# Local attention: transposes ahead of the scores and the projection ahead of the values on the tensor engine

## The reference, cut to what matters

```
q = rmsnorm((x @ wq.T).reshape(B, T, 16, 64), q_norm_w)
k = rmsnorm((x @ wk.T).reshape(B, T, 4, 64), k_norm_w)
v = (x @ wv.T).reshape(B, T, 4, 64)
scores = q . k / sqrt(64), -inf where not (i >= j and i - j < 64)
y = softmax(scores) . v
x = x + y.reshape(B, T, 1024) @ wo.T      # the x on the right of @ above is layernorm(x)
```

## Time and profile before

| what | us |
|---|---|
| median of 3 runs | 2483.01 (2477.14 to 2483.77) |
| the profiled execution, its own time | 2484.49 |
| its span, first to last instruction | 2482.6 |
| PE busy | 2057.6 (83%) |
| DVE busy | 1849.0 (74%) |
| POOL busy | 1429.4 (58%) |
| ACT busy | 1399.7 (56%) |
| local attention, first projection to last addition to x | 1523.9 to 2058.0 |

### The profile page before, as it was taken

How to read it: one execution, slowest core, us unless ns; L and a number is a source line. 1 busy time by engine, 2 the same in 40 slices (tenths; PEclk the granted TensorE clock), 3 DMA queues, 4 the chain that set the end, 5 groups by cost and what they waited for, 6 DMA issues and landing times. The chain is left out here.

```text
span 2482.6 us, 44194 instructions
## 1 busy us (share of the span) xinstructions
PE 2057.6 (83%) x13760; PEld 1290.2 (52%) x13760; DVE 1849.0 (74%) x2871; ACT 1399.7 (56%) x2582; POOL 1429.4 (58%) x1094
## 2 busy tenths in 40 slices
PE   3888888888888886999865894888888888999486
PEld 1334443334333333677643783555555556777476
DVE  5999999999999997577644343777887775776545
ACT  4657676666666662466543452555555564665254
POOL 4788888777888886233244464455555543332646
PEclk7999999999999999799987897999999998999588
DMA  4222222222222221200111220000000001000342
GB/s 121 74 76 72 75 77 73 71 73 70 73 72 75 76 74 43 73 11 11 31 39 50 82 82 27 10 9 8 8 8 8 5 1 56 11 11 7 133 155 73
DMA packets 104423, 130.71 MB, mean 53 GB/s; under 512 B 33668, under 2 KB 65718, under 8 KB 103632
## 3 DMA queue, kind: packets, MB, share of 16 engines
q1 hardware_dynamic: 95600, 111.19, 15.4%
q0 software_dynamic: 8192, 17.59, 2.0%
q10 hardware_dynamic: 512, 0.53, 0.1%
HBM read 111.16 MB, written 25.20 MB: 55 GB/s over the span
## 5 line engine op out<-in xcount | busy, mean ns | idle before, releaser
L829 POOL TENSOR_TENSOR m_hc<-m_h,m_cs 128x1024 f32<-128x1024 f32 x256 | 602.6, 2358 | 183.1 <-DVE m_h L739 167.8
L739 DVE TENSOR_TENSOR_SCAN m_h<-m_da,m_pdb 128x1024 f32<-128x1024 f32 x256 | 585.2, 2286 | 27.5 <-DVE m_pdb L711 3.9
L432 PE MATMUL m_py<-m_hc,ident 128*128 128x512 f32 x1024 | 506.2, 618 | 1.9 <-POOL m_hc L829 1.9
L614 ACT ACTIVATE m_da<-m_dt,m_aneg 128x508 f32<-128x508 f32 x512 | 331.7, 709 | 118.1 <-DVE m_h L739 102.6
L711 DVE TENSOR_TENSOR m_pdb<-m_du,m_pdb 128x1024 f32<-128x1024 f32 x256 | 309.1, 1207 | 26.6 <-PE m_pdb L419 17.5
L432 PEld LDWEIGHTS m_py<-m_hc,ident 128*128 128x128 f32 x1024 | 200.2, 198 | 222.8 <-issue 214.3
L1082 ACT ACTIVATE x_prT<-x_pt 77x512 f32<-77x512 f32 x256 | 138.0, 586 | 139.3 <-PE x_pt L984 138.6
L2077 POOL TENSOR_TENSOR d_r<-d_mean_sq,minus_half 128x20 f32<-128x20 f32 x32 | 113.6, 3549 | 171.7 <-DVE d_mean_sq L2048 171.7
L1198 POOL TENSOR_TENSOR x_kd<-x_kT,x_hm 128x308 f32<-128x308 f32 x64 | 45.0, 703 | 278.5 <-ACT x_v_raw L1094 278.5
L419 PE MATMUL m_pdb<-m_bcrow,m_sel 96*128 96x512 bf16 x256 | 101.2, 396 | 112.6 <-DVE m_h L739 112.6
L2069 POOL TENSOR_TENSOR d_pr<-d_pr,d_rden 128x512 f32<-128x512 f32 x128 | 130.4, 1039 | 49.9 <-DVE d_rden L1991 49.9
(11 more groups left out here) (308 smaller groups left out, 4541.0 us busy)
## 6 DMA issues: line engine op xcount, KB each, us to landing
m_cs<-crow SPq DMA_DIRECT2D x256, 256.0 KB, 3.1
f_row<-f_sorted SPq DMA_DIRECT2D x24, 400.0 KB, 3.3
c_row<-c_sorted SPq DMA_DIRECT2D x40, 144.0 KB
d_back<-c_routed SPq DMA_DIRECT2D x32, 128.0 KB
f_sorted<-in_F_blank SPq DMA_DIRECT2D x9, 400.0 KB
cw_gud<-in_C_gud SPq DMA_DIRECT2D x1, 3456.0 KB
x<-in_x SPq DMA_DIRECT2D x8, 256.0 KB, 4.8
fw_w<-in_F_w SPq DMA_DIRECT2D x1, 2048.0 KB, 8.5
```

The source lines that it names most:

```text
L432: ins = mm(py[:, c, :], S.ident[:, :], hc[n % BUF][:, c, :], start=False, stop=n == NS - 1)
L614: A_(dst, src, ACT.Exp, scale=aneg[:, d, c, n:n + 1]).then_inc(s["da_ready"], 1)
L739: V.tensor_tensor_scan(h[n % BUF][:, way], da[n % BUF][:, d:d + CH * GT][:, way], pdb[:, b:b + 2, :].rearrange("p c t -> p (c t)")[:, way] ...
L829: P.tensor_tensor(hc[n % BUF][:, :, :], h[n % BUF][:, :].rearrange("p (c t) -> p c t", c=CH), bc(cs[n % BUF][:, :], 1, CH), ALU.mult).then ...
```

## The change

On PE, in every slot, the code of slot 2 (transposes of queries and keys) and of slot 3 (projection) moves up to stand right behind the turn. In slot 2 the order is now turn, transposes, scores, values; it was turn, scores, values, transposes. In slot 3 it is now turn, projection, values; it was turn, values, projection. Slots 0 and 1 keep their order. Waits move with the blocks to which they belong. No instruction is added or removed, and the other engines' code is untouched.

```diff
                     nxt, m, n, o = (b.plus(k) for k in (1, 2, 3, -1))
-                    if nxt.real() and q % 2 == 0:
-                        scores(nxt, q // 2)
-                    if q == 1 and n.real():
...
-                    last = b if q else o
-                    if last.real():
-                        values(last, (q - 1) % NQ)
-                    if q == 1 and o.real():
...
                     if q == 2 and m.real():
                         pe.wait_ge(s["qn_ready"], 2 * (m.n + 1))
...
                         mm(pkv[:, :], xT[:, :], W.wkv[:, :], start=True, stop=True).then_inc(s["qkv_mm"], 1)
+                    if nxt.real() and q % 2 == 0:
+                        scores(nxt, q // 2)
+                    if q == 1 and n.real():
...
+                    last = b if q else o
+                    if last.real():
+                        values(last, (q - 1) % NQ)
+                    if q == 1 and o.real():
...
```

More of the change, by code:

```diff
@@ L1903, in slot @@
                         mm(pkv[:, :], xT[:, :], W.wkv[:, :], start=True, stop=True).then_inc(s["qkv_mm"], 1)
+                    if nxt.real() and q % 2 == 0:
+                        scores(nxt, q // 2)
+                    if q == 1 and n.real():
+                        pe.wait_ge(s["xh_ready"], n.n + 1)
+                        if due(n.n - 4):
+                            pe.wait_ge(s["x_ready"], n.n - 4)
+                        tr(px[:, 0:T], xh[:, 0, :], S.ident[:, :]).then_inc(s["t_mm"], 1)
+                    last = b if q else o
+                    if last.real():
+                        values(last, (q - 1) % NQ)
+                    if q == 1 and o.real():
+                        pe.wait_ge(s["cT_ready"], NQ * (o.n + 1))
+                        if due(o.n):
+                            pe.wait_ge(s["x_ready"], o.n)
+                        if n.real():
+                            pe.wait_ge(s["xT_ready"], n.n + 1)
+                        for i in range(NP):
+                            ins = mm(px[:, T:2 * T], cT[o.p][:, i, :], W.wo[:, i, :], start=i == 0, stop=i == NP - 1)
+                        ins.then_inc(s["o_mm"], 1)
                 walk_sequences(pe, slot, 5)
```

## The result

The changed kernel takes 2447.59 us in the median of 4 runs (2442.64 to 2449.27), the kernel before 2480.60 us beside it: a ratio of 0.9864, 95% interval 0.9842 to 0.9886, so 33 us less, with about 5 us to either side. The direction and the mechanism were as forecast; the size was not: 2459 was named, with a range of 2451 to 2469. The profiled execution went from 2484.49 to 2447.85 us, its span from 2482.6 to 2446.0. Where the 36.6 us are, by the two traces: 33.0 in the 28 periods, 2.2 in the start of the layer, 0.5 at its end, and the remaining 1 us outside it.

A forecast was written before the change was run, and what follows sets the result against it. A loop through several engines, none full, was taken as the bound: 15.89 us per period, to become 14.98. Saved 25.5, less 1.1 at the start, plus 0.4 at the end: 24.8 us, so 2458.2, named 2459; range 2451 to 2469.

The forecast's parts named there:

- the 28 periods: One layer's PE order, repeating once per sequence, from the mark behind projection 3 to that behind 31; 15.89 us each before.
- The loop of 7.15 + 8.72: Old period: 7.15 us from mark to slot 2's turn, released by POOL, then 8.72 of PE to the next mark.
- "DVE finishes it at 1793.01, +8.19": DVE finishes `qn` 8.19 us after the mark, so PE's transposes start at +8.29 after a new 0.65 us wait.
- PE's marks: Mark E: on PE, the start of the turn that follows a projection; the periods are counted between these.
- the forecast of 14.98: New period in us: 8.29 + 1.37 + 1.62 + 0.58 + 0.44 + 2.68, which is 0.91 less than 15.89.
- the 25.5 predicted: Saving in us over the periods between marks 3 and 31: 28 x 0.91.
- Hand-over of 0.10 and blocks of 6.69: DVE's `qn` to PE's transposes takes 0.10 us; PE's blocks from the transposes' start to the next mark take 6.69.
- Cover of the copies, of the exponential and of `top`: `qT`/`kT` copies out at +10.52, before the projection at +12.30; exponential 0.55 us in hand; `top`'s delay absorbed by DVE idle time.
- Start +1.1: Layer's start costs 1.1 us: first projection about 2.0 late (bounds +1.3 to +3.9), about 0.9 given back before mark 3.
- End: One more wait for `cT` goes outside the 28 periods: -0.4 us, bounds 0 and -0.9.
- The clock: Rival: new waits lower PE's clock in the loop; 3 periods cost 20 us, all 28 cost 162 more; chance 0.02.
- 2458.2: Forecast median in us: 2459.7 for the profiled execution, less 1.5 because the runs' median is that much below it.

The follow-up runs named there:

- The two halves done alone: Kernel before with only slot 2's transposes moved up: period 15.55 us, ratio 0.9958; with only slot 3's projection moved up: 15.00 us, 0.9908.
- the copy beside it: Changed kernel plus one unused DVE copy (128x512, f32) per sequence, behind the sum of squares' scaling: 2451.05 us, period 14.927 us.
- the written-out loop: Changed kernel with DVE's hardware loop of this layer written out in full: 2376.81 us on another chip, 0.9822 of the kernel before.

## Why the prediction was wrong in size and right in kind

- *The loop of 7.15 + 8.72 and what leaves it.* Right. The block of values and the wait for `cT` are off the path, one wait for `qn` has come. The two halves done alone gave 0.34 and 0.89 us.
- *"DVE finishes it at 1793.01, +8.19".* This is the step that failed, and only in size. I read DVE's stretch in one period of before, and it was the longer of two. The next period of before, from the same timeline:

```profile
1801.31 1.49 DVE L2044 TENSOR_REDUCE d_ssq<-d_sq 128x20 f32<-128x1280 f32 x1 [2.31 <-ACT d_sq L1959]
...
1807.38 1.28 DVE L2009 TENSOR_TENSOR d_qn<-d_pq,d_r 128x512 f32<-128x512 f32 x2
```

  From 1801.31 to the end of `qn` at 1808.66 are 7.35 us, against 7.58 in the period I used. In the old order nobody waited for `qn`, so the difference was invisible in PE's marks (15.87 and 15.94). I had taken the old period as a mean over 28 and the new one from a single sample of an engine that was not yet the bound. Four of the 28 periods also lie outside the hardware loop, where the stretch is 7.12 us: they came out at 14.43 three times and 14.07 (the last has no addition, and a stretch of 6.64). Against the forecast of 14.98, the 24 periods in the loop, at 14.775, give 4.9 us and these four 2.6: the 7.5 us by which the 33.0 of the periods exceed the 25.5 predicted. About 5 of them come from DVE's stretch, the rest from the next point.
- *Hand-over of 0.10 and blocks of 6.69.* The hand-over was 0.05 to 0.06, the blocks 6.73; and since the values now follow the projection, the mark lies 0.09 us later behind its end, so that the sum of squares starts 0.52 after the mark, not 0.61. Together 0.09 us in each period, 2.5 us in all: even with the right stretch the forecast would have been that much too high.
- *Cover of the copies, of the exponential and of `top`.* Right. The only waits of PE in the period are those for `xT`, POOL and `qn`. The 2.23 us for the copies were 0.12 short, as the half with the projection alone showed; here they had 1.6 us in hand. DVE's idle time ahead of the sum of squares fell to 1.31 us, not 1.8: the 2.73 it was counted from was the longer of two (the other is the 2.31 above), and the period fell further.
- *Start +1.1.* The two blocks ahead of the first turn took 5.62 us from PE's release (1551.63 to 1557.25), for 5.61 predicted, but the release came about 1 us before the forecast 1552.6, and as a whole the start's sign can't be told, as shown above. *End.* -0.5 for -0.4.
- *The clock.* 1.00 in both periods, with three waits in each as before, but shorter ones. The rule of the Trainium skill that was weighed (TensorE: Matmul & The Clock Gate, A second HAM failure mode: psum-queue depth-cycling) did not come into play here: no pattern of these short waits, 0.15 to 0.87 us over all the kernels, lowered the clock in the loop.
- *The range.* It took in hand-over, start and the runs' spread, but nothing for the length of DVE's stretch, the one term that became the bound. The 11.4 us from 2459 to the measured 2447.6 add up as follows: 7.5 in the periods; 2.4 because the median of before came out lower with one more run (2480.60 for 2483.01); 0.7 for a start and end that were forecast to cost that much and by the medians cost nothing; 0.8 from naming 2459 for 2458.2. The error in the periods alone would have led to 2451.5, just inside the range; the rest, scatter for the most part, took the time out of it.

## What to carry to other kernels

When a change makes the path run over an engine that had slack before, read that engine's stretch over many periods, not one: while it had slack, its variations were hidden, and gaps between its instructions become part of the period. Moving a block off the path is worth its length plus the wait ahead of it, until the next loop up; work out that floor too. And look at what stands inside the new critical stretch without need: here one addition of 0.28 us, moved into idle time, gave 0.45 us per period.

## What the runs showed of the hardware

- An instruction of DVE can cost more or less than its length. In the hardware loop the addition of 0.28 us cost 0.45 to 0.54, and a copy of 0.42 us at the same place cost 0.19; in sequences written out it was 0.31 and 0.37. That the waits' own instructions fill the gaps of the loop is supported by the written-out loop (stretch of 7.12 us instead of 7.36 and 7.58), but no run took single waits away.
- With the copy beside it POOL's power instruction took 3.64 to 3.72 us in all 32 sequences, and 3.54 to 3.56 in every other kernel, that with the copy ahead of the sum of squares included; the turn of slot 2 waited 0.32 us instead of 0.16. Why it takes longer is not shown:

```profile
1800.58 3.71 POOL L2080 TENSOR_TENSOR d_r<-d_mean_sq,minus_half 128x20 f32<-128x20 f32 x1 [4.00 <-DVE d_mean_sq L2049]
```

- Hand-overs, from the end of one record to the start of the next: 0.14 us from ACT to PE, before `values` (`cT`) and before the projection (`kT`) alike; 0.05 to 0.06 from DVE to PE; 0.08 from POOL to PE.
